# Building layer 1's one-hot selectors during layer 0 and keeping them in DRAM, with node values split into three bf16 parts

## The reference, cut to what matters

```python
xb  = einsum('ei,bio->ebo', h[src], weight)          # 16 bases
msg = einsum('eb,ebo->eo', w_comp[etype], xb)
x_hat = h[src] @ A1_w.T + A1_b
y_hat = h[dst] @ A2_w.T + A2_b + rel_emb[etype]
a = tanh(relu(sum(x_hat * y_hat, -1) / sqrt(32)))
nei = segment_sum(a[:, None] * msg, dst)             # then the self loop and relu
```

## Time and profile before

| | us |
|---|---|
| median of 3 runs (10157.7 to 10171.14) | 10165.41 |
| the profiled execution | 10155.89 |
| its span | 10154.0 |
| POOL busy | 6668.1 (66%) |
| DVE busy | 4403.6 (43%) |
| PE busy | 4395.6 (43%) |
| ACT busy | 2227.0 (22%) |

### The profile page before, as it was taken

How to read it: one execution, slowest core, us unless ns; L and a number is a source line. 1 busy time by engine, 2 the same in 40 slices (tenths; PEclk the granted TensorE clock), 3 DMA queues, 4 the chain that set the end, 5 groups by cost and what they waited for, 6 DMA issues and landing times.

```text
span 10154.0 us, 102607 instructions
## 1 busy us (share of the span) xinstructions
PE 4395.6 (43%) x23835; PEld 3937.0 (39%) x23836; DVE 4403.6 (43%) x8860; ACT 2227.0 (22%) x5821; POOL 6668.1 (66%) x6577
## 2 busy tenths in 40 slices
PE   4444444444466666666663232222233232332223
PEld 3333333333366666666662222222222222222222
DVE  5444444444377777777773222222222222222222
ACT  0000000000477777777770000000000000000000
POOL 5666666664477777777775666666665666666665
PEclk6555555555655555555555555555555555555555
DMA  3111111111477777777771000000000000000001
GB/s 69 22 22 22 22 22 22 22 22 31 160 219 221 219 219 219 218 219 218 220 217 26 11 11 11 11 11 11 11 11 16 11 11 11 11 11 11 11 11 16
DMA packets 601171, 726.23 MB, mean 72 GB/s; under 512 B 341132, under 2 KB 434892, under 8 KB 597969
## 3 DMA queue, kind: packets, MB, share of 16 engines
q0 software_dynamic: 290064, 544.60, 21.8%
q1 hardware_dynamic: 311081, 181.32, 6.5%
HBM read 685.46 MB, written 40.38 MB: 71 GB/s over the span
## 4 chain that ended last, share of the span: by engine, by line
another core or an unknown queue 35%; issue 24%; POOL 22%; DVE 10%; DMA 3%; ACT 2%; PE 1%; DVEq 1%; POOLq 0%; SPq 0%; ACTq 0%
POOL arena L502 13%; POOL lanes L502 9%; DVE arena L978 3%; DMA lanes<-table,idx 2%; DVE arena L950 2%; DVE arena L942 1%; DVE lanes L942 1%; DVE lastrow L973 1%; ACT arena L699 1%; DMA arena<-table,idx 1%; DVE ps L937 0%; DVE lanes L968 0%; DVE lanes L1086 0%; ACT arena L685 0%
## 5 line engine op out<-in xcount | busy, mean ns | idle before, releaser
L502 POOL DMA_INDIRECT lanes<-table,idx x4764 | 4501.0, 945 | 2652.7 <-issue 1435.1
L1214 PE MATMUL ps<-arena,lanes 128*128 128x128 f32 x9528 | 2429.8, 425 | 4543.4 <-DVE arena L950 1844.0
L1214 PEld LDWEIGHTS ps<-arena,lanes 128*128 128x128 f32 x9528 | 2072.7, 303 | 4878.1 <-issue 4798.9
L502 POOL DMA_INDIRECT arena<-table,idx x1664 | 2049.1, 1231 | 676.9 <-issue 507.0
L551 ACT COPY idx<-tabs 128x4 int32 (+1 forms) x1616 | 303.0, 194 | 6851.8 <-DMA lanes<-table,idx 6698.3
L937 DVE TENSOR_TENSOR ps<-ps,tabs 128x16 f32<-128x16 f32 x1191 | 211.4, 177 | 3458.9 <-remote 3121.0
L1214 PE MATMUL ps<-lanes 128*128 128x32 f32 x3328 | 791.6, 402 | 666.0 <-issue 414.3
L1214 PEld LDWEIGHTS ps<-lanes 128*128 128x128 f32 x3328 | 750.3, 330 | 693.1 <-issue 693.0
L950 DVE TENSOR_TENSOR arena<-lanes,ps 128x512 f32<-128x512 f32 x794 | 543.7, 685 | 985.2 <-DMA lanes<-table,idx 944.6
L1311 PE MATMUL ps<-t,arena 128*128 x3328 | 955.5, 402 | 0.0
L1311 PEld LDWEIGHTS ps<-t,arena 128*128 128x128 f32 x3328 | 859.8, 318 | 0.0
(11 more groups left out here) (201 smaller groups left out, 3028.7 us busy)
## 6 DMA issues: line engine op xcount, KB each, us to landing
arena<-step_rows SPq DMA_DIRECT2D x416, 256.0 KB
lanes<-table,idx POOLq DMA_INDIRECT x4764
arena<-table,idx POOLq DMA_INDIRECT x1664
table<-arena SPq DMA_DIRECT2D x24, 1088.0 KB, 4.9
lanes<-in_edge_attr SPq DMA_DIRECT2D x388, 64.0 KB
table<-h SPq DMA_DIRECT2D x18, 256.0 KB, 2.4
edge_rows<-arena SPq DMA_DIRECT2D x1, 2496.0 KB, 8.4
lanes<-self_loop_table,selfi POOLq DMA_INDIRECT x98
```

Of the source, the lines that this page charges most:

```text
L502: pool.indirect_dma_start(out=to[:, k, u, :], out_offset=None, in_=tableD[l], in_offset=bass.IndirectOffsetOnAxis(ap=idx[:, k, u:u + 1], a ...
L1214: last = mm(ps[:, bass.ds(w[u], rhs.shape[-1])], onehot[:, k, u, :], rhs, start=False, stop=True, skip_group_check=True)
```

## The change

The selectors no longer are made in layer 1. During layer 0 SP loads the step rows into five slots of SBUF (`sel`, in bf16), ACT makes `Abs` and `Relu` of 128x1024 in place, and SP stores each slot, 256 KB, to a DRAM tensor `selD`: 416 lots in all, five a round in the first 20 rounds of layer 0 and four a round in the other 79. In layer 1 SP loads them from `selD` when `yc_done` says that PE has used the last ones. Both selectors are bf16 now, so the y values are split into three bf16 parts before layer 1 (seven casts on ACT, seven subtractions, seven casts, seven subtractions, between ACT and DVE), and PE makes six bf16 matmuls a step in place of three and one in f32. The diff, cut to its core:

```diff
@@ the region of tiles
-        rowb, nodeT (f32), relT (bf16), off (f32)
+        selT = region(LOTS * HB * P, BF16).rearrange("p (h u a e) -> p h u a e", h=LOTS, u=HB, a=2)
+        ylow = arena[:, 19600 - FEAT // 2:].bitcast(BF16)
+        yparts = [two bf16 halves of the tile h, then ylow]
+        sel = arena[:, SEL0:SEL0 + SLOTS * HB * P].bitcast(BF16).rearrange("p (h f) -> p h f", h=SLOTS)
@@ SP, layer 0
+            def attr_lot(i, k, of, at):
+                sp.wait_ge(row_used[k], i + 1)
+                sp.dma_start(attr[:, k], ...).then_inc(attr_loaded[k], 16)
+            def load_steps(n, k):
+                sp.dma_start(sel[:, k], stepsD[bass.ds(n * HB, HB), :].rearrange("s f -> (s f)").partition_broadcast(P)
+                             ).then_inc(steps_loaded[k], 16)
+            def store_selectors(n, i, k):
+                sp.wait_ge(sel_ready[k], i + 1)
+                sp.dma_start(selD[bass.ds(n * P, P), :], sel[:, k]).then_inc(sel_stored[k], 16)
+            def round_of(i, of, at, stored, loaded, stored_at, loaded_at, lots_=LOTS):
+                for k in range(max(lots_, stored, loaded)):
+                    if k < lots_:
+                        attr_lot(i, k, of, at)
+                    if k < stored:
+                        store_selectors(stored_at + k, i - 1, k)
+                    if 0 < k <= loaded:
+                        sp.wait_ge(sel_stored[k - 1], i * 16)
+                        load_steps(loaded_at + k - 1, k - 1)
+                if loaded == max(lots_, stored, loaded):
+                    sp.wait_ge(sel_stored[loaded - 1], i * 16)
+                    load_steps(loaded_at + loaded - 1, loaded - 1)
@@ SP, layer 1
             with sp.Fori(0, C[1]) as i:
                 for k in range(LOTS):
-                    sp.wait_ge(sel_ready[k], i + 1)
-                    sp.dma_start(rowb[:, k]..., stepsD[...].partition_broadcast(P)).then_inc(steps_loaded[k], 16)
+                    sp.wait_ge(yc_done[k], i + 1)
+                    sp.dma_start(selT[:, k]..., selD[bass.ds(i * (LOTS * P) + k * P, P), :]).then_inc(sel_loaded[k], 16)
@@ ACT, layer 0 (k = 0 to 4 in the first 20 rounds, then 0 to 3)
+            def selectors(i, k):
+                act.wait_ge(steps_loaded[k], i * 16 + 16)
+                nc.scalar.activation(sel[:, k], sel[:, k], ACT.Abs, scale=-1.0, bias=part[:, 0:1]).then_inc(off_ready, 1)
+            def close(i, k, n):
+                act.wait_ge(off_ready, n)
+                nc.scalar.activation(sel[:, k], sel[:, k], ACT.Relu, scale=-1.0, bias=ones[:, 0:1]).then_inc(sel_ready[k], 1)
-            lots(0)
+                    selectors(i, k)
+                    next_lot(0, i, k, False)
+                    close(i, k, ...)
@@ ACT, layer 1
-                    if ahead[4]: selector_distances(*ahead[4])      # L678
-                    if ahead[4]: selectors(*ahead[4])               # L685, L687
+            act.wait_ge(p1_biased, BLOCKS)
+            for b in range(BANKS):
+                y_part(b, tf, yparts[0], y_high)
+            for b in range(BANKS):
+                act.wait_ge(y_rest, b + 1)
+                y_part(b, tf, yparts[1], y_mid)
             for b in range(BANKS):
                 transposes(1, b)
-            for k in range(4): selector_distances(0, k); selectors(0, k)
@@ DVE, ahead of the masks of the self loop
+            for b in range(BANKS):
+                dve.wait_ge(y_high, b + 1)
+                tt(yf[:, w], yf[:, w], yparts[0][:, w], ALU.subtract).then_inc(y_rest, 1)
+            for b in range(BANKS):
+                dve.wait_ge(y_mid, b + 1)
+                tt(yparts[2][:, w], yf[:, w], yparts[1][:, w], ALU.subtract).then_inc(y_ready, 1)
@@ PE, edge_terms
-                pe.wait_ge(node_sel_ready[k], i + 1)
-                pe.wait_ge(sel_ready[k], i + 2)
+                pe.wait_ge(sel_loaded[k], i * 16 + 16)
                 for u in range(HB):
                     for part_ in range(3):
-                        mm(ps7[:, u, :], relT[:, k, u, :], relparts[:, part_, :], ...)
-                    last = mm(ps7[:, u, BASES:YC], nodeT[:, k, u, :], yf[:, bass.ds(w[u], D)], ...)
+                        mm(ps7[:, u, :], selT[:, k, u, 1, :], relparts[:, part_, :], ...)
+                    for part_ in range(3):
+                        last = mm(ps7[:, u, BASES:YC], selT[:, k, u, 0, :], yparts[part_][:, bass.ds(w[u], D)], ...)
```

More of the change, by code:

```diff
@@ new lines, in of_five, with of_four @@
+            def of_five(i):
+                return i * SLOTS
+            def of_four(i):
+                return i * LOTS + FIVES
+            sp.wait_ge(tabs_copied, ROWCH + 1)
+            for k in range(SLOTS):
+                load_steps(k, k)
+            round_of(0, edge_attr, 0, 0, 0, 0, 0)
+            with sp.Fori(1, FIVES) as i:
+                round_of(i, edge_attr, i * (BODY * P), SLOTS, SLOTS, i * SLOTS - SLOTS, i * SLOTS)
+            round_of(FIVES, edge_attr, FIVES * BODY * P, SLOTS, LOTS, of_five(FIVES - 1), of_four(FIVES))
@@ L402, in _ @@
+            with sp.Fori(FIVES + 1, MAIN) as i:
+                round_of(i, edge_attr, i * (BODY * P), LOTS, LOTS, i * LOTS + (FIVES - LOTS), i * LOTS + FIVES)
+            sp.wait_ge(tail_ready, 4 * 16)
+            for i in range(MAIN, C[0]):
+                round_of(i, attrD, (i - MAIN) * BODY * P, LOTS, LOTS if i < C[0] - 1 else 0, of_four(i - 1), of_four(i),
+                         LOTS if i < C[0] - 1 else LAST_LOTS)
             for b in range(BANKS):
@@ L617, in lots @@
                     next_lot(l, C[l] - 1, k, True)
-            act.wait_ge(tabs_ready, 2)
-            lots(0)
+            def selectors(i, k):
[3 more added lines that the diff above has]
+                act.wait_ge(off_ready, n)
+                nc.scalar.activation(sel[:, k], sel[:, k], ACT.Relu, scale=-1.0, bias=ones[:, 0:1]
+                                     ).then_inc(sel_ready[k], 1)
+            act.wait_ge(tabs_ready, 2)
+            with act.Fori(0, FIVES) as i:
+                for k in range(SLOTS):
+                    selectors(i, k)
+                    if k < LOTS:
+                        next_lot(0, i, k, False)
+                    close(i, k, i * SLOTS + (k + 1))
+            with act.Fori(FIVES, C[0] - 1) as i:
+                for k in range(LOTS):
+                    selectors(i, k)
+                    next_lot(0, i, k, False)
+                    close(i, k, i * LOTS + (FIVES + k + 1))
+            for k in range(LOTS):
+                next_lot(0, C[0] - 1, k, True)
             linear(0, 0)
@@ L714, in body1, with y_part @@
                     act.wait_ge(onehot_ready[k], i + 1)
+            def y_part(b, of, to, there):
+                nc.scalar.copy(to[:, columns(b)], of[:, columns(b)]).then_inc(there, 1)
+            act.wait_ge(p1_biased, BLOCKS)
[4 more added lines that the diff above has]
+                y_part(b, tf, yparts[1], y_mid)
             for b in range(BANKS):
                 transposes(1, b)
-            for k in range(4):
-                selector_distances(0, k)
-                selectors(0, k)
             for k in range(3):
```

78 lines of the change are left out of this document (35 added, 43 removed).

## The result

| | before | after |
|---|---|---|
| median of 4 runs, us | 10168.27 (10157.7 to 10177.35) | 10336.0 (10311.05 to 10359.97) |
| profiled execution / its span, us | 10155.89 / 10154.0 | 10333.4 / 10331.6 |
| gathers of layer 0, first start to last start | 2377.7 | 2592.8 |
| end of layer 0's last gather to start of layer 1's first | 276.8 | 266.7 |
| gathers of layer 1 | 2630.5 | 2603.8 |

The kernel became slower: ratio 1.0165, 95% interval 1.0139 to 1.0191. Of the 177.6 us between the two spans, layer 0 accounts for +215.1. Layer 1 and the stretch ahead of it gave 26.7 + 10.1 back, in sum about the 34 + 4 that were forecast for them. The rest is small. So the question is what happened in layer 0.

A forecast was written before the change was run, and what follows sets the result against it. The prediction took POOL's stream of gathers and the signals between POOL, DVE and PE as the bound. 10155.9 - 34 - 4 + 12 = 10129.9, plus 9.5 for the median, gave 10139 us; range 10040 to 10270.

The forecast's parts named there:

- 34 + 4: Forecast gains in us: 34 in layer 1 from removing ACT's selectors, 4 between the layers.
- SP and the DMA in layer 0: Layer 0: SP's added loads and stores take 6.3 us of issue a five-slot round; +12 us, bounds 0 and +100.
- POOL needs it three lots (some 15 us) later: Layer 0, ACT: the index copy behind an Abs has some 15 us of slack, so ACT's added work costs 0.
- SP's chain of store and load: Rival, layer 0: waits for stores overfill a five-slot round from a 3.5 us landing; 225 us slower, 10364; chance 0.06.
- the right signs: Layer 0 leaves 1.48 to 1.52 us a gather; for SP, DVE waits for attributes or ACT for step rows.
- the signals of layer 0: Rival, layer 0: added DMAs and ACT instructions slow the gather stream, +100 us in place of +12, 10227; chance 0.20.
- my upper bound: Layer 1: all 52.0 us of POOL's real waits vanish once ACT's selectors go; 34 us was taken.
- the rival on pairs: Rival, layer 1: pair ends shift against the gathers; well, 10040 us, chance 0.15; badly, +110 us, 10249, chance 0.06.
- the 1.20 to 1.26 us of my forecast: Layer 1: the forecast is wrong, by the pairs' shift, if POOL's mean gather leaves 1.20 to 1.26 us.
- the stretch ahead of the layer: Between the layers: later masks against ACT's dropped first selectors and PE's shorter steps; -4 us, bounds -13 and +9.
- ACT in layer 0: Layer 0: two added activations a lot, 945 us in all, fit in ACT's round; cost 0.
- TensorE's shorter steps: PE in edge_terms: six bf16 matmuls take 0.26 us a step against 0.56, hidden behind POOL in the loop; 0.

The follow-up runs named there:

- the dose: Kernel before plus two small transfers a lot on SP in layer 0, whose data nobody waits for: ratio 1.0008, pace 1.502 us a gather.
- the second chip: Both kernels rerun unedited on another chip with late signals: changed against before 1.0165; layer 1 took 2606.1 us against 2623.4.
- layer 1's part alone: Kernel before with only layer 1 loading selectors, from four tiles filled once, and node values split in three: 0.9992 with late signals, 1.0022 without.

## Why the prediction was wrong

**The step that failed** is "SP and the DMA in layer 0": "An issue is 0.373 us, 0.45 with its wait and register moves: 14 x 0.45 = 6.3 us in a round with five slots", from which I took +12, "since neither DVE nor PE nor POOL waits for any of them". It measured +215, and ACT waited 1080.1 us for step rows and DVE 428.3 us for attributes. 0.373 is the price of an SP that stands between its issues, as it did before the change: only 18 of 333 issues took some 0.7 us then, and the 1604 of the earlier trace rows was a single one, at 85.9 us. I read it as the price of any issue. For an SP without such stands, in the stream of gathers, it is another. In the changed kernel, 756 issues in 1600 us, less 5% for waits, make 2.0 us each with all that belongs to them, more than four times my 0.45. By that, 14 are 28 us and 12 are 24 us, against a round of 23.9. The later runs show that 2.0 is an outcome and not a floor, but it tells that the round is full where I had 6.3 us in it. The rows that warned were on the page I had: DVE's stalls of 5 and 10 us "without work". I used them for one rival, and didn't ask whether SP, which has to live in the same stretches, would suffer them too once it had no waits. In the kernel before it had 1248 us of waiting in 2000.

**"POOL needs it three lots (some 15 us) later"** was the second half of that error. The slack of some 15 us behind ACT's `Abs` is there only if SP keeps its schedule. SP doesn't, and each member then waits for the one before it.

**The rival "SP's chain of store and load"** had the right place, and named the right signs; I gave it 0.06. That it also came nearest in time, 10364 against 10336, is luck, for its trigger is not what the loss hangs on. It asked for a landing above 3.5 us, and the stores on the chain of layer 0 lie on both sides of that, from about 1.3 to 4.6 us:

```profile
1479.56 4.01 DMA step_selectors<-arena
...
1583.73 2.24 DMA step_selectors<-arena
```

But SP's waits for them add up to 101 us of 2000, and with 128 bytes a partition the loss stayed. What filled the round was SP's own instructions, which this rival priced at 6.3 us as I did. The Trainium skill's figure for HBM at high load ("DMA: Bandwidth & Descriptors", "Latency and other measured facts"), by which a store would take 4.2 us as an estimate, is near the longer ones; but on the chip without late signals, with 132 GB/s in layer 0 against 103, a store on ACT's queue landed in a median of 2.1 us, so no run shows that load is what makes them long.

**The rival "the signals of layer 0"** had less than half the size, 10227 against 10336. It named the place, a lot of layer 0 above 6.0 us (it was 6.5), and the stalls. But its price was one for each added signal, +100 by a bound from layers 0 and 3, and the dose shows that eight more transfers a round cost 0.1%. The bound was not one either. It scaled the cost of added signals in proportion, from layers in which SP had slack; the cost begins where the slack ends.

**Right in its mechanism, and lucky in its sum,** was layer 1. ACT's selectors were what made POOL wait, and the 52.0 us of waits in the loop all went: my upper bound, where I took 34. Mean gather +13 ns on 1648 takes 21.5 us back, a term that I had at nothing (the direction of the bad side of the rival on pairs, at a fraction of its price, and within the 1.20 to 1.26 us of my forecast). The whole layer is 26.7 us shorter, 17.3 on the second chip. That the stretch ahead of the layer gave 10.1, forecast 4, is within its bounds; on the second chip it gave 2.0. A step of edge_terms takes some 0.2 us, forecast 0.26. ACT in layer 0 as bare time costs nothing on the chip without late signals; with them it costs 0.3%. TensorE's shorter steps brought nothing, as said.

**The forecast as a whole** promised too much even with layer 0 free: layer 1's part alone gives 0.9992, not 0.9974, and its interval reaches past 1. On the chip without late signals it is 1.0022. There was little to win: 1063 us of ACT had cost POOL 52.

## What to carry to other kernels

A queue's price for an issue is not the median of its row. Read minimum and maximum too, and ask in which state the row was taken: an SP that stood between its issues showed 0.37 us for each, 0.45 with all that belongs to it, where one that ran on needed 2.0 us. Before work moves to an engine or queue that "only waits", ask what that waiting absorbs: here 1248 us of SP's waiting hid that its instructions take several times as long when it has no such waits while POOL streams. Chains that go around several in-order queues (store, landing, load, activation, index copy) are costed by the latest of them; if they must be, use fewer and larger transfers, or another queue, which took the loss from 1.65% to about 0.1 and 0.5% here. The Trainium skill says in "Perfetto Trace Analysis", section "DMA Optimizations", that balancing DMAs across the engines that can issue them may help where descriptor generation is the bottleneck. Moving transfers to ACT's queue did help, 0.5% in place of 1.6%, though here all of SP's instructions were slow, waits and register moves too, and not its DMA instructions alone.

## What the hardware showed unexpectedly

**Chips differ by 12% at one kernel.** (Each chip was met once, so whether it is the chip or its state in that hour is not shown.) One chip ran the kernel before in 8929 us; all others took 10026 to 10192 us. On the fast one gathers run at 1.25 us in layers 0, 2 and 3 without a stop, and layer 1 is hardly shorter (2595.6 us in one version there against 2621.4 in the same version on a late chip). Of the 1153 us between these two traces of one version, 1031 lie in layers 0, 2 and 3, in stops of POOL, 95 between layers 0 and 1, and 26 in layer 1. A change is judged differently there: at most 0.25% for parts that cost 1.1% elsewhere.

**Signals are late while gathers stream.** On the other chips, where SP hardly stands between its instructions, most of its instructions take 0.70 us each with 0.7 us between, from some 3 us after gathers begin to come at 1.25 us until they pause. After a wait of some us it does its first instructions at full speed even then. If ACT's queue has the transfers, ACT's queue instructions are slow, and its activations are not (1148 ns as ever). In these stretches an `Abs` can start 0.4 us after the recorded start of the issue of its own rows (3.8 us in others), which cannot be the true order of issue and landing: the records of slow instructions run late by some 3 us, as an estimate from that difference. So the order of two records from such a stretch, and a time of 0.70 us for one instruction, are less sure than their sum over a round. Whether the recording itself has a part in the lateness was not tested.
